# Two-head attention stage of an eight-core layer kernel: the 2048-column exponential split into two 1024-column halves with their own PSUM tiles

## What is computed

```python
xn = layernorm(x)                       # eps 1e-5
# every projection has rank 32: (xn @ basis.T) @ (amp * cos(phase)).T
q, k, v = split_heads(proj_q(xn)), split_heads(proj_k(xn)), split_heads(proj_v(xn))   # 16 heads of 64
attn = softmax(einsum('bhqd,bhkd->bhqk', q, k) * 64 ** -0.5)                          # 2048 x 2048 per head
attn_out = proj_o(merge_heads(attn @ v))
# mixture of experts: 8 experts, top 2, hidden 1408, and a shared expert of hidden 2816
ffn = sum_e combine[:, e] * ((silu(xn @ wg[e]) * (xn @ wu[e])) @ wd[e]) + shared(xn)
out = x + attn_out + ffn
```

## Time and profile before

| | us |
|---|---|
| median of 2 runs | 4159.79 |
| the two runs | 4108.47 and 4211.12 |
| the profiled execution | 3961.62 |
| its span, first to last instruction, on the slowest core | 3960.1 |
| spans of the eight cores in it | 3952.1 to 3960.1 |

### The profile page before, as it was taken

The page is one execution under the profiler, slowest core; times in us unless marked ns, Lnnn a source line. Parts: engine busy times, 40 slices in busy tenths (PEclk is TensorE's granted clock), DMA queues, the critical chain, the costliest instruction groups (busy, mean ns, idle before and its releaser), DMA issues.

```text
span 3960.1 us, 45402 instructions; the slowest of 8 cores (3952.1 to 3960.1 us)
## 1 busy us (share of the span) xinstructions
PE 3080.5 (78%) x13795; PEld 1212.6 (31%) x13795; DVE 1823.1 (46%) x2660; ACT 870.2 (22%) x945; POOL 267.5 (7%) x351
## 2 busy tenths in 40 slices
PE   2444355555554489999999999999999999999996
PEld 1111011111111034343443333434334343344432
DVE  4444534444444445444444555544444455433344
ACT  0222166666665011111111100111111110011100
POOL 1000000000000101100000000111000000011000
PEclk9755599999998599999999999999999999999995
DMA  1000000000000143343333333334333333334205
GB/s 31 26 27 17 0 0 1 1 1 1 1 1 11 20 45 40 36 48 38 33 33 32 33 33 33 36 35 48 43 33 33 33 33 33 33 38 49 26 1 160
DMA packets 254434, 116.01 MB, mean 29 GB/s; under 512 B 233592, under 2 KB 233592, under 8 KB 254208
## 3 DMA queue, kind: packets, MB, share of 16 engines
q0 software_dynamic: 245248, 87.87, 21.1%
q1 hardware_dynamic: 8960, 25.24, 2.0%
HBM read 191.40 MB, written 8.39 MB: 50 GB/s over the span
## 4 chain that ended last, share of the span: by engine, by line
PE 67%; ACT 14%; DVE 10%; issue 6%; DMA 2%; DVEq 1%; POOL 0%; ACTq 0%; SPq 0%; POOLq 0%
PE p_xg L812 20%; PE p_xu L821 19%; PE p_d L854 19%; ACT pTs L636 13%; PE p_st L625 4%; PE p_t L411 2%; DVE acc L862 1%; DMA out<-o 1%; PE p_pj L295 1%; DVE gbuf L836 1%; DVE acc L718 1%; DVE o_heads L680 1%; PE p_a L606 1%; DVE o L905 1%; DMA wdbuf<-w_down 1%
## 5 line engine op out<-in xcount | busy, mean ns | idle before, releaser
L854 PE MATMUL p_d<-gbuf,wdbuf 128*128 128x512 bf16 x3520 | 835.8, 378 | 64.9 <-DVE acc L862 35.1
L812 PE MATMUL p_xg<-xnh_fm,wgbuf 128*128 128x512 bf16 x3520 | 844.2, 383 | 24.0 <-DMA wdbuf<-w_down 24.0
L821 PE MATMUL p_xu<-xnh_fm,wubuf 128*128 128x512 bf16 x3520 | 834.5, 380 | 0.0
L836 DVE TENSOR_TENSOR gbuf<-sgt,p_xu 128x512 bf16<-128x512 bf16 x440 | 302.5, 688 | 977.5 <-PE p_xu L821 977.5
L831 ACT ACTIVATE sgt<-p_xg 128x512 bf16<-128x512 f32 x440 | 262.8, 597 | 2177.5 <-PE p_xg L812 1570.2
L862 DVE TENSOR_TENSOR acc<-acc,p_d 128x512 f32<-128x512 f32 x896 | 617.3, 689 | 258.8 <-PE p_d L854 243.1
L636 ACT ACTIVATE pTs<-p_st,bias 128x2048 bf16<-128x2048 f32 x256 | 503.6, 1967 | 337.6 <-PE p_st L625 328.0
L812 PEld LDWEIGHTS p_xg<-xnh_fm,wgbuf 128*128 128x128 bf16 x3520 | 346.3, 99 | 448.4 <-issue 40.7
L821 PEld LDWEIGHTS p_xu<-xnh_fm,wubuf 128*128 128x128 bf16 x3520 | 345.5, 98 | 419.4 <-issue 7.4
L854 PEld LDWEIGHTS p_d<-gbuf,wdbuf 128*128 128x128 bf16 x3520 | 285.1, 96 | 611.1 <-issue 391.8
L625 PE MATMUL p_st<-q_fm,k_fm 64*128 64x512 bf16 x1024 | 162.2, 392 | 311.6 <-ACT pTs L636 311.2
(11 more groups left out here) (200 smaller groups left out, 1025.5 us busy)
## 6 DMA issues: line engine op xcount, KB each, us to landing
wgbuf<-w_gate POOLq DMA_DIRECT2D x88, 256.0 KB, 13.1
wubuf<-w_up POOLq DMA_DIRECT2D x88, 256.0 KB, 14.4
wdbuf<-w_down POOLq DMA_DIRECT2D x88, 256.0 KB, 15.3
x_tm<-x SPq DMA_DIRECT2D x16, 512.0 KB, 3.9
x<-x SPq DMA_DIRECT2D x16, 512.0 KB, 4.4
out<-o SPq DMA_DIRECT2D x16, 512.0 KB, 5.2
wgbuf<-sw_gate POOLq DMA_DIRECT2D x22, 256.0 KB, 10.4
wubuf<-sw_up POOLq DMA_DIRECT2D x22, 256.0 KB, 11.2
```

The source lines that it names most:

```text
L812: emit("tensor", lambda te, buf=buf, loc=loc, c=c, tg=tg: te.matmul(p_xg[:, :], wgbuf[buf][:, loc * 1024 + c * 128: loc * 1024 + c * 128 + ...
L821: emit("tensor", lambda te, buf=buf, loc=loc, c=c, tg=tg: te.matmul(p_xu[:, :], wubuf[buf][:, loc * 1024 + c * 128: loc * 1024 + c * 128 + ...
L836: emit("vector", lambda v, gs=gslice, ss=ss: v.tensor_tensor(gs, sgt[ss][:], p_xu[:, :], ALU.mult), waits=[("t", t_xu), ("s", s_silu)] + ( ...
L854: first=(li == 0), last=(li == len(grp) - 1): te.matmul(pb[:, :], wdbuf[buf][:, li * 1024 + dc * 128: li * 1024 + dc * 128 + 128], gbuf[bu ...
```

## The change

The single score tile is split. `p_stA` has four banks and holds the scores of head hA in two slots of 1024 columns, used in turn from step to step. `p_stB` has two banks and holds the scores of hB in a single slot. `p_c` is gone, and its place in the output projection is taken by the first bank of `p_stB`; all eight banks are used now. The one exponential over 2048 columns becomes two over 1024 columns, first hA's, then hB's, each with waits of its own. The four score matmuls are still emitted in the order A j0, B j0, A j1, B j1, but A j0 waits only for the slot of `p_stA` used two steps ago (`st_freeA[pp]`), and B j0 for the exponential of hB one step ago (`st_freeB`). The value matmuls of each head wait for the exponential of that head alone. The core of the diff:

```diff
-    p_c = pt("p_c", [128, 512], F32, st2p)
-    p_st = pt("p_st", [128, 2048], F32, stx)
+    p_stA = pt("p_stA", [128, 2048], F32, stx)
+    p_stB = pt("p_stB", [128, 1024], F32, stx)
...
-    pTs_free = {0: ("t", 0), 1: ("t", 0)}
+    pTs_free = {(si, pp): ("t", 0) for si in (0, 1) for pp in (0, 1)}
...
-                            waits=([("s", exp_done[p2])] if (sidx == 0 and j == 0) else []) +
+                            waits=([("s", exp_done[sidx][p2])] if j == 0 else []) +
...
-                pTs_free[pp2] = ("t", cnt["t"])
+                    pTs_free[(sidx, pp2)] = ("t", cnt["t"])
...
+                t_spA = t_spB = 0
                 for j in (0, 1):
-                    for sidx, h in ((0, hA), (1, hB)):
...
+                    kc = 2 * pair + j
+                    emit("tensor", lambda te, c8=c8A, off=offA, kc=kc, qb=qb,
+                         pp=pp, j=j: te.matmul(
+                             p_stA[:, pp * 1024 + j * 512: pp * 1024 + j * 512 + 512],
...
+                        waits=(st_freeA[pp] if j == 0 else []) +
...
+                    t_spA = cnt["t"]
+                    emit("tensor", lambda te, c8=c8B, off=offB, kc=kc, qb=qb,
+                         j=j: te.matmul(
+                             p_stB[:, j * 512: j * 512 + 512],
...
+                        waits=(st_freeB if j == 0 else []),
+                        incs=[("t", 1)])
+                    t_spB = cnt["t"]
                 emit("scalar", lambda s, pp=pp: s.activation(
-                    pTs[:, pp * 2048: pp * 2048 + 2048],
-                    p_st[:, 0:2048], AF.Exp,
+                    pTs[:, pp * 2048: pp * 2048 + 1024],
+                    p_stA[:, pp * 1024: pp * 1024 + 1024], AF.Exp,
                     scale=0.125, bias=bias128[:]),
-                    waits=[("t", t_sp), pTs_free[pp]], incs=[("s", 1)])
+                    waits=[("t", t_spA), pTs_free[(0, pp)]], incs=[("s", 1)])
+                st_freeA[pp] = [("s", cnt["s"])]
+                exp_done[0][pair] = cnt["s"]
+                emit("scalar", lambda s, pp=pp: s.activation(
+                    pTs[:, pp * 2048 + 1024: pp * 2048 + 2048],
+                    p_stB[:, 0:1024], AF.Exp,
+                    scale=0.125, bias=bias128[:]),
+                    waits=[("t", t_spB), pTs_free[(1, pp)]], incs=[("s", 1)])
+                st_freeB = [("s", cnt["s"])]
+                exp_done[1][pair] = cnt["s"]
...
-    pbc_free2 = {0: ("v", v_onorm), 1: ("v", v_onorm)}
+    pbc_free2 = {0: [("v", v_onorm)] + list(av_free[1]),
+                 1: [("v", v_onorm)] + list(st_freeB)}
...
-            pbank = p_b if slot == 0 else p_c
+            pbank = p_b[:, :] if slot == 0 else p_stB[:, 0:512]
```

More of the change, by code:

```diff
@@ L589, in build_nc @@
     rrow_free = [("dr0", 0), ("dr1", 0)]
-    st_free = [("s", s_p1_done), ("v", v_p1_done)]
+    st_freeA = {0: [("s", s_p1_done), ("v", v_p1_done)],
+                1: [("s", s_p1_done), ("v", v_p1_done)]}
+    st_freeB = [("s", s_p1_done), ("v", v_p1_done)]
     av_free = {0: list(pa_free), 1: list(pbc_free[0])}
-    pTs_free = {0: ("t", 0), 1: ("t", 0)}
+    pTs_free = {(si, pp): ("t", 0) for si in (0, 1) for pp in (0, 1)}
     pairs = [(2 * hp, 2 * hp + 1, qb) for hp in range(NHEAD // 2) for qb in range(NTG)]
     for mi, (hA, hB, qb) in enumerate(pairs):
-        exp_done = [0] * 8
+        exp_done = {0: [0] * 8, 1: [0] * 8}
         for pair in range(10):
@@ L615, in build_nc @@
                             incs=[("t", 1)])
-                pTs_free[pp2] = ("t", cnt["t"])
+                    pTs_free[(sidx, pp2)] = ("t", cnt["t"])
             if pair < 8:
                 pp = pair % 2
-                first = True
+                c8A, offA = hA // 2, (hA % 2) * 64
+                c8B, offB = hB // 2, (hB % 2) * 64
+                t_spA = t_spB = 0
                 for j in (0, 1):
-                    for sidx, h in ((0, hA), (1, hB)):
[L622 to L634, removed]
@@ L635, in build_nc @@
-                t_sp = cnt["t"]
+                    kc = 2 * pair + j
+                    emit("tensor", lambda te, c8=c8A, off=offA, kc=kc, qb=qb,
+                         pp=pp, j=j: te.matmul(
+                             p_stA[:, pp * 1024 + j * 512: pp * 1024 + j * 512 + 512],
+                             k_fm[off:off + 64, c8 * T + kc * 128: c8 * T + kc * 128 + 128],
+                             q_fm[off:off + 64, c8 * T + qb * 512: c8 * T + qb * 512 + 512],
+                             start=True, stop=True),
+                        waits=(st_freeA[pp] if j == 0 else []) +
+                              ([("v", v_bias)] if (mi == 0 and pair == 0 and j == 0)
+                               else []),
+                        incs=[("t", 1)])
@@ L711, in build_nc @@
             slot = (c8 * NTG + tg) % 2
-            pbank = p_b if slot == 0 else p_c
+            pbank = p_b[:, :] if slot == 0 else p_stB[:, 0:512]
             emit("tensor", lambda te, c8=c8, tg=tg, pb=pbank: te.matmul(
-                pb[:, :], wT["o"][:, c8 * 128:(c8 + 1) * 128],
+                pb, wT["o"][:, c8 * 128:(c8 + 1) * 128],
                 res_bf[:, tg * 512: tg * 512 + 512], start=True, stop=True),
-                waits=[("s", s_reso), pbc_free2[slot]], incs=[("t", 1)])
+                waits=[("s", s_reso)] + pbc_free2[slot], incs=[("t", 1)])
             t_ao = cnt["t"]
             emit("vector", lambda v, c8=c8, tg=tg, pb=pbank: v.tensor_copy(
-                acc[:, c8 * T + tg * 512: c8 * T + tg * 512 + 512], pb[:, :]),
+                acc[:, c8 * T + tg * 512: c8 * T + tg * 512 + 512], pb),
                 waits=[("t", t_ao)], incs=[("v", 1)])
-            pbc_free2[slot] = ("v", cnt["v"])
+            pbc_free2[slot] = [("v", cnt["v"])]
     v_acc0 = cnt["v"]
```

2 lines of the change are left out of this document (removed).

## The result

The changed kernel is slower: the ratio of its time to that of the kernel before is 1.0175, with a 95% interval of 1.0162 to 1.0188. By the bound of 2% that is no clear change; by its own interval it is a clear loss of 70 us. In some executions of either kernel cores were granted a lower clock in part of the span (a mean as low as 0.79 over the span, against 0.90 to 0.92 otherwise), and the ratio leaves those out.

The account below looks back on a forecast made before the run. In attention, ScalarE's exponentials and TensorE's score matmuls wait for each other in turn, neither the bound alone. Steps +53.8, unit ends +1, last values -0.4, low clock -3, lone waits +2.3: +54 us on 4159.8 gives 4214, range 4010 to 4270.

Parts of the forecast that it names:

- The loop: Attention steps: A j1 stands behind B j0's wait, so hA's exponential cannot start before hB's last one has ended.
- half an exponential: ScalarE in attention: an exponential of 1024 columns takes 1.113 us, two 2.226 us, 0.26 more than the whole.
- gap between the halves: ScalarE between hA's and hB's exponentials: 0.20 us, bounds 0.147 and 0.29.
- idle time before hA's: ScalarE before hA's exponential: falls from 0.92 to 0.70 us, one pair of score matmuls on the path instead of two.
- ordinary step: Attention step inside a unit: 3.126 us against 2.887, +0.24 us, over 224 steps +53.8 us.
- idle time at a unit's end: ScalarE at a unit's end: 1.46 us instead of 1.89, step 3.89 against 3.86 us, 31 ends +1 us.
- lone waits of 0.28 us: Attention stage: extra idle of 0.29 us once in 32 exponentials, sixteen instead of eight if following instruction count, +2.3 us.
- the number of low-clock steps: Attention steps at the lower TensorE clock: 14 assumed, each growing +0.03 instead of +0.24 us, together -3 us.
- the three by which it called itself wrong: Attention: hA's exponential starting under 0.5 or over 0.85 us after hB's end, or halves under 1.0 us.
- The clock: Rival: longer TensorE idle in a unit's second step holds 1.2 GHz through the attention stage, +47 us, 4261 us; chance 0.09.
- The pair that does not run side by side: Rival: A j1 starts only as B j0 ends, 0.22 us more a step, +103 in all, 4263 us; chance 0.08.
- not slower: Rival: A j1 executes without waiting for B j0, attention step 2.63 us, -58 us, 4102 us; chance 0.03.

Follow-up runs that it names:

- one_slot: The changed kernel with hA's scores using one slot of p_stA in every step; ratio 1.0182 to the kernel before, attention stage 839.8 to 842.5 us.
- a_first: The changed kernel with score matmuls ordered A j0, A j1, B j0, B j1; ratio 0.9803 to the kernel before, attention stage 758.3 to 761.1 us.
- filler9: The changed kernel with nine surplus A j0 score matmuls in each unit's second step; attention stage 830.2 to 833.5 us, no ratio given.

## Why the prediction was right and where it was off

**The loop: right.** That B j0's wait holds A j1, and that hA's exponential therefore cannot start before hB's has ended, stands in the chain (709.44 to 710.14) and in the counts (251.6 us of waiting on `p_stB`, 0.4 on `p_stA`). one_slot and a_first show it from both sides: the second slot is worth nothing in this order, and the order alone is worth 0.5 us a step.

**The terms of the step: right.**

| term | forecast | measured |
|---|---|---|
| half an exponential | 1.113 us | 1.113 |
| gap between the halves | 0.20 | 0.203 |
| idle time before hA's | 0.70 | 0.70 |
| ordinary step | 3.126 | 3.133 |
| idle time at a unit's end | 1.46 | 1.43 |
| lone waits of 0.28 us | 16 | 16 |

With the estimate of 1.133 us for a half from the Trainium skill's figures ("ScalarE: Activation LUTs", What ACT_TABLE_LOAD costs) the trace does not quite agree: 1.113, as taken from the rows. The Trainium skill's rule that matmuls start and end in program order ("TensorE: Matmul & The Clock Gate", Part 3) holds by the records where the forecast needed it: A j1 never started ahead of the waiting B j0 (2048 steps on the eight cores, at the earliest 5 ns behind it). It does not hold in general: in a_first hB's first score matmul, with nothing left to wait for, started before A j1 (703.37 against 703.77).

The sixteen lone waits of 0.28 us were counted in ScalarE's timeline, all before hB's exponential at a unit's end, one in every second unit: 56.4 - 256 x 0.203 = 4.4 us. That they go with the number of instructions issued is borne out by the doubling; what they are was not tried.

**The failed step in the change itself: the number of low-clock steps.** The sum kept the 14 of the kernel before (there were 16) and booked them as a gain of 3 us, since such a step grows by only 0.03. In the changed kernel there are 60, and each is 0.21 us longer than an ordinary one: (60 - 14) x 0.21 = 9.7 us. The two unit ends at the low clock add 2 x 0.87 = 1.7, and the 0.007 us by which the step was short 1.6. Together 13; the unit ends came out at 3.85 us and not 3.89, which is 1 less, and leaves the 66.1 - 54 = 12 by which the stage missed the forecast. Of the signs that the forecast gave, the granted clock of at least 0.95 (it was 0.87) and the stage of 831 us (842.5) failed; none of the three by which it called itself wrong came. filler9 takes the low clock away: its stage is 830.2 to 833.5 us, and the forecast's sum without its low-clock steps (14 x 0.21 = 3 us) and with the measured step is 776.4 + 54 - 3 + 1.6 = 829.

The prediction had seen the mechanism, as its rival "The clock", and had worked out that TensorE's idle piece in a unit's second step grows from 2.30 to 2.54 us (it was 2.51). Its mistake was to price it as all or nothing: +47 us at a chance of 0.09, or the 14 steps of before and no more. The trace of the kernel before had steps of both kinds in the same place: 10 of 32 units with low-clock steps at their start and 22 without. So a count between was possible, up to the first two or three steps of every unit, and that is what came. The forecast also looked to the idle piece itself, which one_slot refutes as the cause.

**The other 4 to 6 us** lie behind the stage. The output projection's first part shows it in the chain of the changed kernel:

```profile
1392.16 3.59 PE p_a L715 x8
...
1396.67 3.59 PE p_a L715 x8
...
1401.18 3.59 PE p_a L715 x8
...
1405.68 1.90 PE p_a L715 x8
```

Three of four groups of eight matmuls ran at 1.2 GHz on this core; in the kernel before it was one of four on its slowest core (3.57, then 1.90 three times). From the last exponential to the first of the experts' activations it is 143.3 us here and 139.0 there. Over the cores it is 136.2 to 143.5 after and 135.9 to 139.8 before, so at which group the clock rises differs from core to core. The time is the slowest core's: the median of the eight spans grew by 65.7 us, as the stage did, and the span of core 1, the slowest before, by 57.8 us only, to 4017.9. Why the clock rose later on the slowest core was not tried.

**The other rivals.** The pair that does not run side by side is refuted (both start at 709.58). The version in which A j1 need not wait, forecast at 2.63 us a step as the rival "not slower", is what a_first has built: 2.634. Of the changed kernel it was rightly given little.

**The failed step in the stated time: the base.** The forecast put its 54 us on 4159.8 us, the median of two executions, 147 and 250 us above the profiled one. Five executions of the kernel before took 3960.6 to 3963.3, so that base is 198 us too high; less the 16 us by which the change was taken too small, this makes the 181 us between 4214 and 4033, but for rounding. The forecast saw it coming, since its range begins at 4010: on the profiled execution the same sum gave 4016, against 4033.5 measured. The verdict "within 2%" was given 0.78 and holds, at the upper end of the forecast's own +15 to +82.

## What to carry to other kernels

A second buffer helps only if the whole group of instructions that fills it stands ahead of the wait for the other buffer in the engine's list; here one matmul behind that wait made it worthless. Splitting one ScalarE instruction into two has a price that the existing rows give to 1% (here 0.26 us of fixed part and 0.20 us of gap), and it has to be earned back in full by work that leaves the path. And when a change lengthens stretches in which TensorE has little to do, look in the trace for how often the clock falls there already, and give the forecast a term for more of the same steps, not for none or all. Last, put a forecast on the execution whose trace was read, and not on a median of a few scattered ones.

## What the runs showed of the hardware

- Surplus matmuls made the stage shorter: nine useless ones in each unit, 288 in all, took 11 us off the stage of the changed kernel, and five in each unit 5 us off that of the kernel before, by keeping the clock at 2.4 GHz (0.99 and 1.00 in the stage).
- It was not the idle piece in itself that brought the clock down: cut from 2.5 to 1.4 us by moving one matmul (one_slot), it left 55 to 62 low-clock steps where 57 to 60 had been. More matmul work in the same place removed them (59, 24, 3 on core 4 with none, five, nine). Which measure of work decides is left open.
- What a low clock costs depends on what TensorE has under cover: 0.21 us a step in the changed kernel, 0.42 in the kernel before, 1.27 in a_first, at the same two levels.
- A matmul behind a waiting one never started ahead of it (0 of 2048 steps of the changed kernel), but where neither waited, two matmuls on different partitions did not start in the order of the list: in 64 of 256 steps of a_first the third of four started ahead of the second, by up to 0.40 us, nearly always beside the first.
